# Rotary products of a slot-attention layer at full width: one matrix product for one half of two heads, the sum of two products in one double add, and the halves put in place by transfers

## The reference, cut to what matters

```
def _rope(x, cos, sin):
    x1, x2 = jnp.split(x, 2, axis=-1)
    return jnp.concatenate([x1 * cos - x2 * sin, x2 * cos + x1 * sin], axis=-1)
q = (hs @ Wq.T).reshape(B, T, H, DK)          # H = 16, DK = 128
k = (hs @ Wk.T).reshape(B, T, H, DK)
q = _rope(q, cos, sin).transpose(0, 2, 1, 3)
k = _rope(k, cos, sin).transpose(0, 2, 1, 3)
v = (hs @ Wv.T)...;  g = (hs @ Wg.T)...
s = clip(hs @ Ws1.T @ Ws2.T + bs2)            # 64 slots a head
z = cumlogsumexp(s);  es = exp(s);  enz = exp(-z)
A = mask(q @ k.T * DK ** -0.5)
qv = softmax(enz * (A @ es))
W2 = mask((qv * enz) @ es.T)
o = W2 @ v
out = (rms_norm(o) * g * sigmoid(g)) @ Wo.T
```

## Time and profile before

| | before |
|---|---|
| median of 3 runs | 719.83 us (719.68 to 726.68) |
| profiled execution, span | 722.0 us |
| PE busy | 634.3 us (88%) |
| DVE busy | 564.7 us (78%) |
| ACT busy | 393.4 us (54%) |
| POOL busy | 282.6 us (39%) |
| mean granted TensorE clock | 0.958 of full |

### The profile page before, as it was taken

The page is one execution under the profiler, slowest core; times in us unless marked ns, Lnnn a source line. Parts: engine busy times, 40 slices in busy tenths (PEclk is TensorE's granted clock), DMA queues, the critical chain, the costliest instruction groups (busy, mean ns, idle before and its releaser), DMA issues. The chain is left out here.

```text
span 722.0 us, 14685 instructions
## 1 busy us (share of the span) xinstructions
PE 634.3 (88%) x4272; PEld 524.0 (73%) x4272; DVE 564.7 (78%) x1270; ACT 393.4 (54%) x1023; POOL 282.6 (39%) x269
## 2 busy tenths in 40 slices
PE   2887999999999999999999985489999987789996
PEld 1666888888788888888888875255556543689996
DVE  6876997988979979979979877788888962364444
ACT  2344555554474565465456443268888865635553
POOL 3453636545535546546366333533343310210000
PEclk9998999999999999999999999579999988889999
DMA  6000201002002002002010000500000000000001
GB/s 217 30 0 1 74 0 47 27 0 73 0 0 73 0 0 73 0 0 73 0 59 1 1 2 13 221 2 1 1 1 0 0 1 0 1 1 0 0 0 58
DMA packets 9295, 18.98 MB, mean 26 GB/s; under 512 B 1968, under 2 KB 5296, under 8 KB 9008
## 3 DMA queue, kind: packets, MB, share of 16 engines
q1 hardware_dynamic: 9264, 18.60, 7.5%
HBM read 17.55 MB, written 1.05 MB: 26 GB/s over the span
## 5 line engine op out<-in xcount | busy, mean ns | idle before, releaser
L741 ACT ACTIVATE sa_v<-bank 128x256 f32<-128x256 f32 x64 | 24.6, 385 | 80.8 <-PE bank L179 80.0
L808 POOL TENSOR_TENSOR sa_kt<-sa_rope_cos,sa_rope_sin 128x512 f32<-128x512 f32 x32 | 41.6, 1299 | 58.1 <-DVE sa_rope_sin L659 58.1
L1430 DVE SCALAR_TENSOR_TENSOR ff_hid<-bank,ff_scale,ff_act_out 128x128 f32<-128x128 f32 x72 | 25.2, 351 | 46.8 <-ACT ff_act_out L1513 43.6
L177 PE MATMUL bank<-sa_vg_hi,ht_hi 128*128 128x512 f32 x128 | 53.0, 414 | 5.2 <-DVE sa_rope_sin L659 3.6
L808 POOL TENSOR_TENSOR sa_qt<-sa_rope_cos,sa_rope_sin 128x512 f32<-128x512 f32 x32 | 41.3, 1290 | 38.7 <-DVE sa_rope_sin L659 38.7
L177 PE MATMUL bank<-ht_hi,sa_qk_hi 128*128 128x512 f32 x128 | 54.7, 427 | 0.8
L814 POOL TENSOR_TENSOR sa_qe<-sa_ex,sa_enz 128x256 f32<-128x256 f32 x32 | 23.4, 730 | 73.8 <-ACT sa_ex L717 73.8
L179 PE MATMUL bank<-ht_hi,sa_qk_lo 128*128 128x512 f32 x128 | 50.7, 396 | 0.0
L178 PE MATMUL bank<-sa_vg_lo,ht_hi 128*128 128x512 f32 x128 | 50.6, 395 | 0.0
L179 PE MATMUL bank<-sa_vg_hi,ht_lo 128*128 128x512 f32 x128 | 50.5, 395 | 0.0
L178 PE MATMUL bank<-ht_lo,sa_qk_hi 128*128 128x512 f32 x128 | 50.5, 395 | 0.0
(11 more groups left out here) (215 smaller groups left out, 2101.4 us busy)
## 6 DMA issues: line engine op xcount, KB each, us to landing
sa_qk_raw<-in_wqk SPq DMA_DIRECT2D x8, 512.0 KB, 5.0
sa_vg_raw<-in_wvg SPq DMA_DIRECT2D x8, 512.0 KB, 3.5
w_raw<-in_w SPq DMA_DIRECT2D x1, 2304.0 KB, 12.1
sa_wo_raw<-in_wo SPq DMA_DIRECT2D x8, 256.0 KB, 3.6
w<-in_w SPq DMA_DIRECT2D x1, 1152.0 KB, 13.9
xs<-in_x SPq DMA_DIRECT2D x2, 512.0 KB, 4.7
out<-xs SPq DMA_DIRECT2D x4, 256.0 KB, 2.4
sa_ws_raw<-in_ws SPq DMA_DIRECT2D x1, 512.0 KB, 6.6
```

Source lines behind the costliest of these rows:

```text
L177: pe.matmul(out, w_hi, m_hi, start=first, stop=False)
L808: pool.tensor_tensor(dst[:, h, c * HALF:(c + 1) * HALF], rope_cos[:, s, :], rope_sin[:, s, :], ALU.add).then_inc(roped, 1)
```

## The change

The wide axis of a projection's result was "all 128 channels of one head"; it becomes "64 channels (one half, `half`) of both heads", rows 0 to 63 head 0, rows 64 to 127 head 1. So x1 and x2 of the rotation are the results of two successive steps QK 2m and QK 2m + 1, row against row. m // 2 is the half of the tokens, m % 2 is q or k.

- The weights are loaded in that order of columns: `load_qk` makes four transfers of 128 KB where one of 512 KB was, each row of them in pieces of 64 elements (256 bytes).
- DVE makes two products of full width for each QK step: with the cosine, and with the sine or its negative (`signed_sin`; the constants get 128 more columns), the latter into the other half's place of `rope_sin`. `rope_cos` and `rope_sin` are doubled.
- POOL adds once for two steps, 1,024 elements a row, into `turned`, which lies in the buffer `hn`, free by then. It does so at QK 1, 3, 5, 7.
- SP then issues four transfers for each m (`place`), each 64 partitions x 512 elements (128 KB) from `turned` to the right half of the rows of `qt` or `kt`. They count `roped`, now two semaphores; A 0 and A 2 wait for both.
- SP's loop is written out. In each turn `place` for m = 0 to 3 stands between the load of `wo_raw` and that of `qk_raw`.
- All orders are set anew. On PE QK 0 and ST 0 now stand between A 0 and E 0, QK 1 between A 1 and E 1, and CS 0 before Y 3. The four late projections before VG 2 are QK 5, 6, 7 and ST 1. The last pass's orders are as before.

```
-PE_ORDER = [("A", 0), ("E", 0), ("A", 1), ("QK", 0), ("ST", 0), ("E", 1), ("T", 0), ("A", 2), ("W", 0), ("QK", 1),
-    ("O", 0), ("E", 2), ...
+PE_ORDER = [("A", 0), ("QK", 0), ("ST", 0), ("E", 0), ("A", 1), ("QK", 1), ("E", 1), ("T", 0), ("A", 2), ("W", 0),
+    ("SN", 0), ("E", 2), ("T", 1), ("A", 3), ("O", 0), ("QK", 2), ("VG", 0), ("W", 1), ("QK", 3), ("E", 3),
+    ("O", 1), ("T", 2), ("QK", 4), ("VG", 1), ("T", 3), ("W", 2), ("SN", 1), ("OT", 0), ("W", 3), ("QK", 5),
+    ("QK", 6), ("O", 2), ("Y", 0), ("QK", 7), ("O", 3), ("OT", 1), ("ST", 1), ("VG", 2), ("VG", 3), ("VG", 4),
+    ("Y", 1), ("OT", 2), ("VG", 5), ("VG", 6), ("OT", 3), ("Y", 2), ("VG", 7), ("CS", 0), ("Y", 3), ("CS", 1)]
+DVE_ORDER = [("A", 0), ("QK", 0), ("E", 0), ("A", 1), ("ST", 0), ("SUM", 0), ("E", 1), ("A", 2), ("QK", 1),
+    ("W", 0), ... ]
+ACT_ORDER = [("W2P", 0), ("E", 0), ("VGHI", 0), ("T", 0), ("WOHI", 0), ("E", 1), ("O", 0), ("T", 1), ("VG", 0),
+    ("E", 2), ("T", 2), ("E", 3), ("ST", 0), ("SN", 0), ("T", 3), ("VG", 1), ("O", 1), ... ("OT", 3),
+    ("VG", 6), ("QKHI", 0), ("VG", 7), ("CS", 0), ("CS", 1)]
+POOL_ORDER = [("WO", 0), ("E", 0), ("VGLO", 0), ("E", 1), ("QK", 1), ("MS", 0), ("E", 2), ("QK", 3), ("E", 3),
+    ("MS", 1), ("WOLO", 0), ("QK", 5), ("SN", 0), ("MS", 2), ("QK", 7), ("MS", 3), ("SN", 1), ("QKLO", 0)]
...
+            def load_qk(r):
+                for kc in range(KC):
+                    for h in range(2):
+                        sp.dma_start(qk_raw[:, kc, :].rearrange("p (m h d) -> p m h d", h=2, m=4)[:, :, h, :],
+                                     a["wqk"][r][:, kc, h * 256:(h + 1) * 256].rearrange("p (m d) -> p m d", m=4)).then_inc(qk_in, 16)
...
+            def place(r, m, attended):
+                c, dst = m // 2, (qt, kt)[m % 2]
+                sp.wait_ge(rope_sum, 4 * r + m + 1)
+                if attended:
+                    sp.wait_ge(a_ready, at(r - 1, 2 * c + 1))
+                for h in range(2):
+                    for half in range(2):
+                        sp.dma_start(dst[64 * half:64 * half + 64, h, c * HALF:(c + 1) * HALF],
+                                     turned[64 * h:64 * h + 64, m % 2, half, :]).then_inc(roped[m % 2], 16)
+            for i in range(PAIRS - 2):
                 sp.wait_ge(vg_lo_done, i + 2)
                 sp.dma_start(vg_raw[:, :, :], a["wvg"][i + 2]).then_inc(vg_in, 16)
                 sp.wait_ge(wo_scaled, i + 2)
                 sp.dma_start(wo_raw[:, :, :], a["wo"][i + 1]).then_inc(wo_in, 16)
+                for m in range(4):
+                    place(i + 1, m, True)
                 sp.wait_ge(qk_lo_done, i + 2)
-                sp.dma_start(qk_raw[:, :, :], a["wqk"][i + 2]).then_inc(qk_in, 16)
+                load_qk(i + 2)
...
                         if g % 2 == 0:
-                            pe.wait_ge(roped, 8 * i + 4 * (g // 2) + 4)
+                            for placed in roped:
+                                pe.wait_ge(placed, 64 * (2 * i + g // 2 + 1))
...
-                        dve.tensor_tensor(rope_cos[:, s, :]..., psv, cos4, ALU.mult)
-                        dve.tensor_tensor(rs[0:64], psv[64:128], sin4[64:128], ALU.mult)
-                        dve.tensor_tensor(rs[64:128], psv[0:64], sin4[0:64], ALU.mult).then_inc(drain, 1)
+                        dve.tensor_tensor(rope_cos[:, m % 2, half, :]..., psv, cos4, ALU.mult)
+                        dve.tensor_tensor(rope_sin[:, m % 2, 1 - half, :]..., psv, sin4, ALU.mult).then_inc(drain, 1)
...
-            act.wait_ge(qk_in, 16)
+            act.wait_ge(qk_in, 64)
             act.activation(qk_hi[:, :, :], qk_raw[:, :, :], ACT.Copy).then_inc(qk_hi_done, 1)
             norm.scalar(act)
...
-                        pool.tensor_tensor(dst[:, h, c * HALF:(c + 1) * HALF], rope_cos[:, s, :], rope_sin[:, s, :],
-                                           ALU.add).then_inc(roped, 1)
+                        if attend or m >= 2:
+                            pool.wait_ge(roped[m % 2], 64 * (2 * r + m // 2))
+                        pool.tensor_tensor(turned[:, m % 2, :, :], rope_cos[:, m % 2, :, :], rope_sin[:, m % 2, :, :],
+                                           ALU.add).then_inc(rope_sum, 1)
```

More of the change, by code:

```diff
@@ L40 @@
 C_TRI, C_TRIS, C_ID, C_COS, C_SIN, C_ONE, C_FREQ, C_BEFORE, C_LOW_W, C_LOW_U = 0, 128, 256, 384, 512, 640, 641, 645, 709, 710
-C_ALL = C_LOW_U + 1
+C_MINUS_SIN = C_LOW_U + 1
+C_ALL = C_MINUS_SIN + TOK
 def constants():
@@ L54, in constants @@
     c[:, C_COS:C_COS + TOK] = np.concatenate([cos, cos])
-    c[:, C_SIN:C_SIN + TOK] = np.concatenate([sin, -sin])
+    c[:, C_SIN:C_SIN + TOK] = np.concatenate([sin, sin])
+    c[:, C_MINUS_SIN:C_MINUS_SIN + TOK] = -np.concatenate([sin, sin])
     c[[S_RANK, QUAD + S_RANK], C_ONE] = 1.0
@@ L307, in slot_attention @@
     tri, tris = con[:, C_TRI:C_TRI + TOK], con[:, C_TRIS:C_TRIS + TOK]
-    ident, cos, sin = con[:, C_ID:C_ID + P], con[:, C_COS:C_COS + TOK], con[:, C_SIN:C_SIN + TOK]
+    ident, cos = con[:, C_ID:C_ID + P], con[:, C_COS:C_COS + TOK]
+    signed_sin = con[:, C_SIN:C_SIN + TOK], con[:, C_MINUS_SIN:C_MINUS_SIN + TOK]
     with ExitStack() as ctx:
@@ L390, in _ @@
             sp.wait_ge(qk_lo_done, 1)
-            sp.dma_start(qk_raw[:, :, :], a["wqk"][1]).then_inc(qk_in, 16)
+            load_qk(1)
             sp.wait_ge(vg_lo_done, 1)
             sp.dma_start(vg_raw[:, :, :], a["wvg"][1]).then_inc(vg_in, 16)
-            with sp.Fori(0, PAIRS - 2) as i:
+            def place(r, m, attended):
[8 more added lines that the diff above has]
+            for m in range(4):
+                place(0, m, False)
+            for i in range(PAIRS - 2):
                 sp.wait_ge(vg_lo_done, i + 2)
@@ L398, in _ @@
                 sp.dma_start(wo_raw[:, :, :], a["wo"][i + 1]).then_inc(wo_in, 16)
+                for m in range(4):
+                    place(i + 1, m, True)
                 sp.wait_ge(qk_lo_done, i + 2)
-                sp.dma_start(qk_raw[:, :, :], a["wqk"][i + 2]).then_inc(qk_in, 16)
+                load_qk(i + 2)
             sp.wait_ge(wo_scaled, PAIRS)
             sp.dma_start(wo_raw[:, :, :], a["wo"][PAIRS - 1]).then_inc(wo_in, 16)
+            for m in range(4):
+                place(PAIRS - 1, m, True)
             sp.dma_start(early["wkv"][:, :], a["wkv"]).then_inc(early["par_in"], 16)
@@ L510, in run @@
                     elif step == "QK":
-                        c, j = n // 4, n % 4
+                        c, m, half = n // 4, n // 2 % 2, n % 2
                         if n == 0:
                             pe.wait_ge(qk_lo_done, r + 1)
-                        cols, w = slice(c * HALF, (c + 1) * HALF), slice(j * DK, (j + 1) * DK)
+                        cols, w = slice(c * HALF, (c + 1) * HALF), slice((2 * m + half) * P, (2 * m + half + 1) * P)
                         for kc in range(KC):
@@ L649, in run @@
                     elif step == "QK":
-                        if attend or n >= 2:
-                            dve.wait_ge(roped, 8 * r + n - 1)
+                        m, half = n // 2, n % 2
+                        if half == 0 and (attend or n >= 4):
+                            dve.wait_ge(rope_sum, 4 * r + m - 1)
                         cos4 = cos.unsqueeze(1).to_broadcast([P, 4, TOK])
-                        sin4 = sin.unsqueeze(1).to_broadcast([P, 4, TOK])
+                        sin4 = signed_sin[half].unsqueeze(1).to_broadcast([P, 4, TOK])
                         psv = bank(ps, 0, 512, 4)
-                        rs = rope_sin[:, s, :].rearrange("p (b t) -> p b t", b=4)
-                        dve.tensor_tensor(rope_cos[:, s, :].rearrange("p (b t) -> p b t", b=4), psv, cos4, ALU.mult)
-                        dve.tensor_tensor(rs[0:64], psv[64:128], sin4[64:128], ALU.mult)
-                        dve.tensor_tensor(rs[64:128], psv[0:64], sin4[0:64], ALU.mult).then_inc(drain, 1)
+                        dve.tensor_tensor(rope_cos[:, m % 2, half, :].rearrange("p (b t) -> p b t", b=4), psv, cos4, ALU.mult)
+                        dve.tensor_tensor(rope_sin[:, m % 2, 1 - half, :].rearrange("p (b t) -> p b t", b=4), psv, sin4,
+                                          ALU.mult).then_inc(drain, 1)
                     elif step == "VG":
@@ L709, in run @@
                     elif step == "QKHI":
-                        act.wait_ge(qk_in, 16 * r + 32)
+                        act.wait_ge(qk_in, 64 * r + 128)
                         act.wait_ge(fill, filled(r, ("QK", 7)))
```

28 lines of the change are left out of this document (11 added, 17 removed), and 19 rows, old and new, of tables (ACT_ORDER, DVE_ORDER, PE_ORDER).

## The result

The changed kernel takes 737.38 us (median of 4 runs, 736.16 to 739.43) where the kernel before takes 720.02 (4 runs, 719.68 to 726.68): a ratio of 1.0214, 95% interval 1.0163 to 1.0266. It is slower by 2.1%; the forecast was 701.7.

A forecast was written before the change was run, and what follows sets the result against it. PE, busy 48.2 of 51.0 us, was taken to bound the loop, DVE close behind. Loop 9.6, pass 0 3.5, first pass 2.5 and start-up 2.5 made 18.1 us off 722.0; less 2.2, 701.7; 8-in-10 range 692 to 713.

The forecast's parts named there:

- the one headed POOL: Loop passes: POOL's adds, fewer but twice as long, stay hidden; 0 us a pass, between -0.5 and +1.
- the second rival: Loop: DVE pays for the double adds, 1 us a pass over seven, giving 708.7 us; chance 0.13.
- The sum of the loop pass: Loop passes 1 to 6: new waits of 2.6 us replace 3.9; 1.6 us gain taken, 49.5 us a pass.
- PE's own work: Loop pass on PE: some 47.2 us without waits, below which no order can make a pass shorter.
- T 3's wait: Loop pass on PE: a small wait of 0.5 us, as POOL's double add stands before its `qe`.
- the third rival: Loop gives nothing, new orders waiting as much as the old; only earlier stages count: 712 us, chance 0.10.
- the ST 0 wait: Loop pass: PE stands 1.6 us before ST 0 for ACT's `ws2_pair`, with E 0 queued behind it.
- The start-up: Before the slot product: later weights let `hn` finish before POOL's `qk_lo` starts; 2.5 us less.
- two of the signs that I had named for being wrong: Profile after: `hn` still showing 4 us, or DVE's small instructions having grown, would show the forecast wrong.
- The first pass: Slot product to A 0: lighter DVE lets PE lead, 29.6 us becoming 27.1; gain 2.5, between 0 and 3.5.
- Pass i = 0: Pass 0: QK 0 moves into PE's idle stretch before the clock falls; gain 3.5 us, between 1.5 and 5.
- the slower rival: Loop: Q/K weights land late behind placing transfers and hold ACT; 5 us late gives 732 us; chance 0.06.

The follow-up runs named there:

- a2: Changed kernel with VGLO computed on only 4 of 512 columns after the first pass, the rest left out: 722.05 us, ratio 0.9983 to the kernel before.
- a5: Changed kernel with ST 0 behind A 1 on PE and VGLO behind E 1 on POOL, nothing left out: 710.76 us, ratio 0.9873 to the kernel before.
- a1: Changed kernel with ST 0 on PE moved from before E 0 to after A 1: 727.62 us, ratio 1.0067 to the kernel before.
- b3: Changed kernel with all lists of the kernel before and the Q/K load ahead of the placing transfers: 713.09 us, ratio 0.9876.
- c1: Changed kernel with the edits of a5, b1, b2 and c3 together: 702.63 us, ratio 0.9726 to the kernel before.
- b2: Changed kernel with each double add on POOL split into two adds of 512 elements: 726.68 us, ratio 1.0089 to the kernel before.
- b1: Changed kernel with POOL's first `qk_lo` waiting for all eight `hn`: 735.07 us, ratio 1.0190 to the kernel before.
- c4: Kernel before with POOL's first `qk_lo` waiting for all eight `hn`: 717.01 us, ratio 0.9923 to the unedited kernel before.
- c3: Changed kernel with POOL taking QK 3's add ahead of SN 0 in a reordered first-pass list: 733.91 us, ratio 1.0158 to the kernel before.
- a3: Changed kernel with double adds on 4 of 512 elements of each half, the rest left out: 717.89 us, ratio 0.9925 to the kernel before.
- a4: Changed kernel with placing transfers after the first pass cut to 8 of 512 elements a row: 738.00 us, ratio 1.0225 to the kernel before.
- c2: b3 with double adds split in two and the first `qk_lo` behind all eight `hn`: 709.76 us, ratio 0.9776 to the kernel before.

## Why the prediction was wrong

**The step that failed** is the one headed POOL: "Twice as long an add may mean longer waits, half as many: I take 0, with ends of -0.5 and +1 us a pass." The mechanism was named there and in the second rival, but two things were mis-sized, and the term came out at some 2.7 us a pass, 16 us in the six.
- Only the adds were priced. VGLO was not: the change takes away the QK 0 add that stood ahead of it, and moves WO and ACT's VGHI forward, so POOL starts VGLO right behind `qe` of group 0, beside DVE's sum of that group and ahead of E 1, and no longer 3.8 us after the sum. This costs 2.1 us a pass (a2; a5 against a1). I followed each added step of POOL's list, and not those that moved because one ahead of them went. That the missing add alone already does harm, at another place, is what b3 shows.
- The adds count by their length and by whom they meet, not by their sum. POOL's total fell (282.6 to 275.6 us) while DVE's held time rose from 2.0 to 6.8 us a pass. With VGLO out of the way the doubling of the adds costs 0.56 us a pass (c1 against a5), inside my bound of 1; beside VGLO, 1.5 (b2). DVE busy came out at 43.5 us a pass, not 39.6; without the 6.8 it would be 36.7.

**The sum of the loop pass.** I had 49.5 and it was 53.64: 2.1 from VGLO and 0.56 from the adds leave 1.5. PE's own work was too low: c1's 49.37 us pass with 0.94 and 0.56 of waits, start against start, leaves 47.9, not 47.2. Most of the other 0.8 is a wait that I hadn't found, QK 3's for its bank (0.55 us by the profile in the pass at full clock). T 3's wait I had, but with the wrong cause: it is DVE's L624, held to 245.49, that makes ACT and then POOL's `qe` late, and not POOL's add in the queue. By this sum the forecast orders, with VGLO elsewhere and the adds not doubled, would have taken some 51 us, which is the third rival ("the new orders wait as much as the old"), not the forecast; no run has just that. c1 has the pass of the forecast, 49.3, because it gave up the ST 0 wait.

**The start-up.** -2.5 became 0 because the weights had landed by 10.6 again. I had added 2.0 us to the landing for the four issues and the small pieces. The issue of `ws_raw` let SP go after 1.21 us instead of the 2.04 of the earlier trace rows, the four issues took 3.74 us, and the last 128 KB, issued at 7.3, was there 3.3 us later. My mechanism was right: when `hn` comes first (b1, c4) the slot product is at 16.0, and I had 16.9. Its trigger was wrong; the change doesn't pull it. That `hn` still shows 4 us and that DVE's small instructions have grown were two of the signs that I had named for being wrong.

**The first pass.** The forecast of -2.5 had DVE's saving in full and overlooked what queues on POOL behind `es_lo`. c3 gives 2.0 of it back.

**Pass i = 0.** -3.5 became +0.7. PE stands 3.96 us before ST 0, and E 0 behind it, but that isn't what took the gain: with ST 0 late the pass still lasts 56.80 (a1) and 56.90 us (a5), where it was 57.29. It is shorter where POOL's work beside DVE is: 55.60 with a tiny VGLO (a2), 54.82 with split adds (b2), 54.08 with tiny adds (a3). These three have a mean clock of 0.97 in that pass and a1 and a5 have 0.94; but b1, whose passes are those of the changed kernel, has 0.97 and 57.07 us, so the clock alone doesn't make the difference. Which of the held steps does wasn't followed up. In b3, with the old orders, the pass is 3.0 shorter than before, at 0.97, and in c2 1.7, at 0.94.

**Right:** ST 0 waits (1.61 by the profile, 1.77 start against start; `ws_pair` ready at V + 6.2 as computed); two products a QK step at 685 ns; no wait before the first O; the placing transfers cost nothing (a4), and the Q/K load behind them lands in time, so the slower rival that I wrote, a late landing, isn't the way it became slower. 512 KB in pieces of 256 bytes and four transfers landed at most 5.1 us after the first issue in the loop (2.3 of issuing and 2.8 to the last landing), where one transfer took 5.0 beside two other loads. With no other load issued near it, from 14.2 in either start-up, the one transfer landed after 3.3 us and the last of the four, issued 1.5 us behind the first, at most 3.0 after its issue, so 4.5. By the rule of the Trainium skill ("DMA: Bandwidth & Descriptors", "Specifications"), which the prediction weighed, I estimated twice the time; neither of the two comparisons shows that.

The rule of the Trainium skill ("SBUF — State Buffer", "SBUF: two separate sides"), that DVE with two SBUF operands and POOL exclude each other for a whole instruction, is what these runs show: L633 in a2 and after, L624 in a3. It is stated for two SBUF operands, and L613 and L684, with one in PSUM, are never held. `hn` has one tensor operand, so this part of the rule doesn't speak of it, and it was held all the same. I cited it and put no price on its worst case, 2.3 us for a step of 0.16.

## What to carry to other kernels

A shorter list for an engine is also a changed time for everything left on it: when a step goes, ask which step behind it was held back by that one, and beside what it now falls. On POOL, long instructions are a cost to DVE by their place and length, even when POOL is idle half the time; keep them away from the chain of small two-operand DVE steps, and cut them where they can't be moved. Test the idea with the old orders before judging it with new ones: here the idea gained 1.2%, its orders lost 3.4%, and with mended orders, split adds and `hn` first the whole is 2.7% faster, of which `hn` first is worth 0.5 to 0.8% without the change. And compare passes at the same granted clock: a mean over six can hide 0.35 us a pass.

## What the runs showed of the hardware

- A DVE step of 4 elements a row takes 0.16 us and up to 2.34 when a POOL instruction is under way; `hn` was held for 4.2 us, through POOL instructions that follow each other (`qk_lo` to 14.16, then the clearing of `es_t` to 15.94), and not let in between. With two short adds (c1, 221.95) a DVE step was let in.
- After the late E 2 (PE busy 0.96 of 2 us) the clock fell to 1.2 GHz (means of 0.90, 0.50 and 0.75 in the three stretches of 2 us from 231), and that cost 0 to 0.4 us a pass where DVE was late anyway, and 1.5 us in a pass of a2; in b3, after a wait of 1.74 us, it stayed there longer (0.75, 0.50, 0.50, 0.54), which cost 2.9 us of one pass, and passes with the same wait went without it.
- A transfer of 128 KB from SBUF to SBUF landed 2.3 us after its issue, of 2 KB 1.7 to 1.8 us. SP needs 0.6 us for one of them.
